# Attention outputs in three fp32r products of halves instead of one fp32 product, in fourteen of sixteen batches

## The reference, cut to what matters

```python
q = softmax_over_the_64_of_a_head(Wq @ layernorm(x)) * SCALE      # 512 x 2048
k = softmax_over_the_2048_columns(Wk @ ctx)                       # 512 x 2048
context = einsum('hdn,hen->hde', k, Wv @ ctx)                     # 64 x 64 per head
out = Wo @ einsum('hde,hdn->hen', context, q) + bo                # 256 x 2048
x = x + out / norm(out, over the 256 rows) * g * sqrt(256)
```

## Time and profile before

| | us |
|---|---|
| median of 3 runs | 2569.74 |
| lowest and highest | 2566.20, 2570.11 |
| profiled execution | 2568.32 |
| its span | 2566.60 |
| mean granted TensorE clock in it | 0.982 of 2.4 GHz |

### The profile page before, as it was taken

How to read it: one execution, slowest core, us unless ns; L and a number is a source line. 1 busy time by engine, 2 the same in 40 slices (tenths; PEclk the granted TensorE clock), 3 DMA queues, 4 the chain that set the end, 5 groups by cost and what they waited for, 6 DMA issues and landing times.

```text
span 2566.6 us, 35379 instructions
## 1 busy us (share of the span) xinstructions
PE 2413.9 (94%) x12004; PEld 1914.3 (75%) x12004; DVE 1726.8 (67%) x4114; ACT 1172.8 (46%) x2464; POOL 1094.4 (43%) x1107
## 2 busy tenths in 40 slices
PE   7999999999999999999999999999999999899774
PEld 6888878887878778787877778777778876777521
DVE  4454567676767557776776567667687756877786
ACT  4454444545354444545444454544445344453333
POOL 1635536172635427262543616245272633623410
PEclk9999999999999999999999999999999999999887
DMA  7112221313122432312213243343302233231376
GB/s 237 50 66 99 74 92 56 108 41 103 63 70 96 128 119 83 113 62 70 95 67 99 80 153 93 120 141 101 123 34 90 92 114 117 76 117 44 88 221 193
DMA packets 200145, 255.72 MB, mean 100 GB/s; under 512 B 43550, under 2 KB 109854, under 8 KB 199966
## 3 DMA queue, kind: packets, MB, share of 16 engines
q1 hardware_dynamic: 199966, 253.47, 31.3%
HBM read 177.53 MB, written 75.89 MB: 99 GB/s over the span
## 4 chain that ended last, share of the span: by engine, by line
PE 57%; DVE 20%; POOL 11%; issue 8%; ACT 3%; SPq 1%; DMA 1%; DVEq 0%; POOLq 0%; ACTq 0%
PE kc_bank L642 15%; PE big L701 7%; PE tb L743 4%; PE tb L757 3%; PE tb L628 3%; PE big L616 3%; PE big L618 3%; PE big L617 3%; POOL x_tr L1535 3%; DVE stats L889 3%; PE big L675 3%; PE big L677 2%; PE big L676 2%; PE tb L686 2%; POOL q_sb L1515 2%
## 5 line engine op out<-in xcount | busy, mean ns | idle before, releaser
L1254 ACT COPY turned<-tb 128x512 f32<-128x512 f32 x512 | 298.7, 587 | 755.3 <-PE tb L686 487.9
L701 PE MATMUL big<-merged,turned 128*128 128x256 f32 x2048 | 495.0, 385 | 36.3 <-ACT turned L1254 24.5
L642 PE MATMUL kc_bank<-ctxt,turned 128*128 128x256 f32 x2048 | 479.5, 380 | 3.0 <-DMA ctxt<-in_ctx_t 3.0
L701 PEld LDWEIGHTS big<-merged,turned 128*128 128x128 f32 x2048 | 385.8, 191 | 110.7 <-ACT turned L1254 19.4
L642 PEld LDWEIGHTS kc_bank<-ctxt,turned 128*128 128x128 f32 x2048 | 374.6, 191 | 54.6 <-issue 8.9
L1490 POOL TENSOR_TENSOR in_l<-x_sb,in_h 128x512 fp32r<-128x512 f32 x128 | 167.8, 1340 | 574.9 <-ACT in_h L1294 574.8
L1515 POOL TENSOR_TENSOR q_sb<-q_sb,qsum 128x1024 f32<-128x1024 f32 x128 | 243.8, 1904 | 274.4 <-DVE qsum L971 274.4
L980 DVE SCALAR_TENSOR_TENSOR on<-big,nrm,g_rows 128x256 f32<-128x256 f32 x256 | 111.9, 479 | 220.7 <-POOL nrm L1528 220.4
L616 PE MATMUL big<-in_h,wk_h 128*128 128x512 f32 x512 | 237.7, 464 | 15.4 <-DVE in_l L821 10.0
L675 PE MATMUL big<-wq_h,in_h 128*128 128x512 f32 x512 | 236.4, 462 | 10.9 <-DVE q_sb L959 10.4
L757 PE MATMUL tb<-mix_ld,mix_w 121*96 121x512 f32 (+2 forms) x324 | 187.9, 677 | 57.7 <-POOL mix_w L1497 28.0
(11 more groups left out here) (149 smaller groups left out, 4308.5 us busy)
## 6 DMA issues: line engine op xcount, KB each, us to landing
mix_ld<-streams SPq DMA_DIRECT2D x157, 240.0 KB
ctxt<-in_ctx_t SPq DMA_DIRECT2D x64, 512.0 KB, 4.0
x_sb<-in_x SPq DMA_DIRECT2D x64, 512.0 KB, 6.1
x_tr<-in_x_t SPq DMA_DIRECT2D x64, 512.0 KB, 6.6
streams<-x_sb SPq DMA_DIRECT2D x64, 512.0 KB, 3.1
stage<-in_ctx SPq DMA_DIRECT2D x60, 512.0 KB, 4.1
out<-mix_out SPq DMA_DIRECT2D x157, 192.0 KB, 2.2
streams<-y_sb SPq DMA_DIRECT2D x32, 256.0 KB, 2.0
```

The source lines that it names most:

```text
L642: t = nc.tensor.matmul(kc_bank[:, 0:C], turned[n % 3][:, j * P:(j + 1) * P], ctxt[:, nt, :], start=nt == 0, stop=nt == NT - 1)
L701: t = nc.tensor.matmul(big[2 + p % 2][:, half], turned[n % 3][:, dt * P:(dt + 1) * P], merged[:, dt, :], start=dt == 0, stop=dt == DT - 1)
L1254: nc.scalar.copy(turned[k % 3][:], tb[n % 2][:]).then_inc(s_tba, 1)
```

## The change

In the first fourteen batches (`SPLIT`) the product of the attention outputs is split. ACT's `turn` writes its copy rounded to fp32r (`turned_h`). DVE's new `query_low` subtracts it from the bank and writes the low half into `q_low`, which lies where `k_exp` lies and of which three quarters are used in turn. `chain_bank` writes a high and a low half of `merged` in three operations instead of one. `attention_out` makes 12 fp32r products of 256 columns instead of 4 in fp32. On DVE `query_low` of tile i−5 stands behind the subtraction of step i; on PE the transposes of tile i−4 now stand ahead of the outputs of tile i−5. A bank with a transposed tile is free once DVE has read it. `key_exp` of the next batch waits for the last outputs, since they read the room of `k_exp`. `pre_t` loses its buffer and uses one of `q_sb`. Batches 14 and 15 go on as before.

```diff
...
+    SPLIT = FIRST[-1]
...
+    LOW_READS = {("fg", b * FG + DT * NQ + i): b * NT + i + 1 for b in range(SPLIT) for i in range(NT)}
...
+        s_low = sem("s_low")
+        s_mrg = sem("s_mrg")
...
-        k_exp = sb("k_exp", [P, N])
-        turned = [sb(f"turned{i}", [P, BANK]) for i in range(3)]
+        with nc.sbuf_tensor("k_exp", [P, N], F32) as k_exp:
+            pass
+        q_low = sb("q_low", [P, 4, BANK], F32R)
+        with nc.sbuf_tensor("turned", [P, 3, BANK], F32) as turned_all:
+            pass
+        turned_h = sb("turned_h", [P, 3, BANK], F32R)
+        turned = [turned_all[:, i, :] for i in range(3)]
...
-        merged = sb("merged", [P, DT, C])
+        with nc.sbuf_tensor("merged", [P, DT, C], F32) as merged:
+            pass
+        merged_h, merged_l = (sb(f"merged_{h}", [P, DT, C], F32R) for h in "hl")
...
-        pre_t = sb("pre_t", [P, COLS])
...
         def f32(ap):
...
+        def low_of(n):
+            return q_low[:, n % 3, :]
+        def pre_t(b):
+            return q_sb[((b + 1) * PAIRS + 2) % QB if b + 1 < NB else QB - 1][:, 0, :]
...
         def wait_read(w, n):
...
-            if name in SCALAR_READS:
+            if name in LOW_READS:
+                w.wait_ge(s_low, LOW_READS[name])
+            elif name in SCALAR_READS:
...
             else:
...
                     else:
...
-                w.wait_ge(s_tba, SCALAR_READS["fg", n])
-                w.wait_ge(s_tbv, VECTOR_READS["chain", b, DT - 1, 2])
-                for dt in range(DT):
-                    t = nc.tensor.matmul(big[2 + p % 2][:, half], turned[n % 3][:, dt * P:(dt + 1) * P], merged[:, dt, :],
-                                         start=dt == 0, stop=dt == DT - 1)
+                bank = big[2 + p % 2][:, half]
+                if b < SPLIT:
+                    w.wait_ge(s_low, LOW_READS["fg", n])
+                    w.wait_ge(s_mrg, 2 * (b + 1) * DT)
+                    for dt in range(DT):
+                        high = turned_h[:, n % 3, dt * P:(dt + 1) * P]
+                        nc.tensor.matmul(bank, high, merged_h[:, dt, :], start=dt == 0, stop=False)
+                        nc.tensor.matmul(bank, high, merged_l[:, dt, :], start=False, stop=False)
+                        t = nc.tensor.matmul(bank, low_of(n)[:, dt * P:(dt + 1) * P], merged_h[:, dt, :], start=False,
+                                             stop=dt == DT - 1)
+                else:
+                    w.wait_ge(s_tba, SCALAR_READS["fg", n])
+                    w.wait_ge(s_tbv, VECTOR_READS["chain", b, DT - 1, 2])
+                    for dt in range(DT):
+                        t = nc.tensor.matmul(bank, turned[n % 3][:, dt * P:(dt + 1) * P], merged[:, dt, :],
+                                             start=dt == 0, stop=dt == DT - 1)
...
             def return_pair(b, p):
...
                         for k in range(KT):
-                            t = nc.tensor.matmul(bank[:], pre_t[:, k * P:(k + 1) * P], wb[:, k, :], start=k == 0,
+                            t = nc.tensor.matmul(bank[:], pre_t(b)[:, k * P:(k + 1) * P], wb[:, k, :], start=k == 0,
...
                     elif task[0] == "mix":
...
                     if i < 2:
...
+                    if 4 <= i < NT + 4 and b < SPLIT:
+                        query_transpose(b, i - 4)
                     if 5 <= i < NT + 5:
...
                     if 10 <= i < NT and i % 2 == 0:
...
-                    if 4 <= i < NT + 4:
+                    if 4 <= i < NT + 4 and b >= SPLIT:
...
                     if b + 1 < NB and i in (17, 19, 21, 23):
...
                 if k == 0:
+                    w.wait_ge(s_mrg, 2 * min(n, SPLIT * DT))
...
                 elif k == 1:
...
                 else:
                     if b:
...
-                    nc.vector.tensor_tensor(merged[:, dt, :], bank[:, 0:C], bo_heads[:], ALU.add).then_inc(s_tbv, 1)
+                    if b < SPLIT:
+                        nc.vector.tensor_tensor(merged_h[:, dt, :], bank[:, 0:C], bo_heads[:], ALU.add).then_inc(s_mrg, 1)
+                        w.wait_ge(s_mrg, 2 * n + 1)
+                        nc.vector.tensor_tensor(chain_t, bank[:, 0:C], f32(merged_h[:, dt, :]), ALU.subtract).then_inc(s_tbv, 1)
+                        w.wait_ge(s_tbv, VECTOR_READS["chain", b, dt, 2])
+                        nc.vector.tensor_tensor(merged_l[:, dt, :], chain_t, bo_heads[:], ALU.add).then_inc(s_mrg, 1)
+                    else:
+                        nc.vector.tensor_tensor(merged[:, dt, :], bank[:, 0:C], bo_heads[:], ALU.add).then_inc(s_tbv, 1)
...
             def key_max(b, dt, i):
...
+            def query_low(b, i):
+                n = b * FG + DT * NQ + i
+                if i == 0:
+                    w.wait_ge(s_tb, TB["fg", n - 1] + 1)
+                w.wait_ge(s_use, n - 2)
+                w.wait_ge(s_tba, SCALAR_READS["fg", n])
+                nc.vector.tensor_tensor(low_of(n), tb[TB["fg", n] % 2][:], f32(turned_h[:, n % 3, :]), ALU.subtract).then_inc(s_low, 1)
             def query_sum(b, p):
...
+                w.wait_ge(s_mrg, 2 * min(b + 1, SPLIT) * DT)
                 if n:
...
                 for j in range(2):
...
                     if i < NT:
...
+                    if b < SPLIT and 5 <= i < NT + 5:
+                        query_low(b, i - 5)
                     if i == 1:
...
                     if i >= 8 and i % 2 == 0 and i < NT + 8:
...
                 if n:
...
+                if b and dt == 0:
+                    w.wait_ge(s_use, b * FG)
...
                 if k >= 3:
...
-                nc.scalar.copy(turned[k % 3][:], tb[n % 2][:]).then_inc(s_tba, 1)
+                if ("fg", k) in LOW_READS:
+                    nc.scalar.copy(turned_h[:, k % 3, :], tb[n % 2][:]).then_inc(s_tba, 1)
+                else:
+                    nc.scalar.copy(turned[k % 3], tb[n % 2][:]).then_inc(s_tba, 1)
...
             def query_exp(b, p):
...
             def pre_out(b, ct):
...
-                nc.scalar.copy(pre_t[:], tb[n % 2][:]).then_inc(s_tba, 1)
+                nc.scalar.copy(pre_t(b), tb[n % 2][:]).then_inc(s_tba, 1)
...
             def y_out(b, ct):
...
```

## The result

| | before | after |
|---|---|---|
| median, us | 2568.18 (4 runs) | 2630.68 (4 runs) |
| lowest and highest | 2566.20, 2570.11 | 2629.41, 2634.49 |
| profiled execution, its span | 2568.32, 2566.6 | 2631.82, 2630.1 |
| mean granted TensorE clock | 0.982 | 0.967 |

The ratio is 1.0246, with a 95% interval of 1.0228 to 1.0264: 62 us more. Forecast was 2597, 29 us more, with 2578 to 2618 as the range of the mechanism that was thought likeliest. The direction holds, and the wait that was named is there; the size is double, because three of its terms were too small.

What follows compares the result with a forecast made beforehand. PE sets the pace with DVE close behind. Twelve batches with Sinkhorn work at 2.7 us late give 32, batches 0 and 1 −3: +29 on 2568.3, so 2597 us; range 2578 to 2618, chance 0.42.

Steps and rivals of the forecast that it cites:

- PE's term: Attention outputs on PE: twelve fp32r matmuls at 0.12 us, 1.44 per tile, saving 0.29 per tile, 65 us if all counts.
- Rival E: The three products on PE are no cheaper; with full weight loads 123 us more than before, 2691; chance 0.04.
- The stage ends 2.7 us late: End of the walk through batch 4's query stage, taken for twelve batches with Sinkhorn work: 12 × 2.7 = 32 us.
- Step 5 … +1.1: Query stage, step 5: operations on merged and the first low half delay the outputs; PE's step ends 1.1 us later.
- I take 7.4: Steps 6 to 9: 7.4 us per pair, between 7.1 and 8.2 with the even stall; PE loses 0.3.
- About +0.3: Steps 10 to 14: DVE 8.45 us per pair against PE's old 8.40; about 0.3 more, late by 1.7.
- Step 15: Step without logits, where PE used to run ahead of DVE and doesn't any more; no cost given.
- low half 14: Steps 16 to 20: it follows second_stats, key_max and a Sinkhorn step on DVE, ends near 720.5; stage 2.7 us late.
- Batches 0 and 1: Query stages where PE stays the bound: 3.2 us saved less 0.4 and 1.3, 1.5 us sooner each, −3 in all.
- B: Rival: VectorE keeps up and the kernel gets faster, 2539, or 2503 with the whole saving; chance 0.32.
- C: Rival: saving and added work cancel, and late outputs 14 are caught up beside the key logits: 2568, within 4; chance 0.12.
- D: Rival: the waits bring TensorE's clock down, 24 to 48 us on top of the forecast, 2621 to 2645; chance 0.10.

Runs made afterwards that it cites:

- e9: Kernel before with only the transposes of tile i-4 put ahead of the outputs of tile i-5, in the first fourteen batches: 2557.7 us.
- e7: Kernel after, but from batch 1 on the low half of merged isn't renewed, one operation per part instead of three: 28 us less.
- e1: Kernel after without the low halves of the queries; the third product reads the high half again: 2568 us.
- e2: Kernel after with low halves made but not read; the outputs wait for ACT alone: 2590 us.
- e10: Kernel before with the outputs of fourteen batches as one fp32r product of high halves, old order, no low halves: gains 50 us.
- e12: Kernel after with unread filler matmuls on PE, sixteen in step 15 and eight in step 19 of batches 2 to 13: 5 us less.
- e14: Kernel after with low half 10 moved to the head of step 15 and low half 14 ahead of second_stats in step 18: 2625 us.

## Why the direction was right and the size wrong

**The accounts of the 62 us.** Order of the transposes −9 (e9), `merged` +28 (e7), DVE's time for the low halves +22, PE's wait for them +41 (e1, e2). What is left to reach e1's +0.5 is 0.5 + 9 − 28 = −18: the cheaper products, where 0.29 × 224 would be 65. This last term is a remainder and takes it that the parts add up. In general they don't: the order alone was worth −9 us on before, nothing in e10 and −70 in after. That PE's time is worth little here has its own evidence in e10's 18% of 280 us and in e12, where 34 us of full-rate time gave 5 to 7.

**PE's term.** The pitch was right. PE in step 8 of batch 4 (start us, us):

```profile
681.63 0.60 PE L709 MATMUL tb<-ident,q_sb 128*128 128x128 f32 x4
683.14 0.38 PE L727 MATMUL big<-merged_h,turned_h 128*128 128x256 f32 x1 [0.91 <-DVE q_low L1015]
683.36 0.28 PE L728 MATMUL big<-merged_l,turned_h 128*128 128x256 f32 x1
...
684.56 0.28 PE L729 MATMUL big<-merged_h,q_low 128*128 128x256 f32 x1
```

Ten matmuls from 683.36 to 684.56 are 0.12 each, the value taken. In batch 0, where nothing holds PE up, a whole step is 3.27 us (from 102.86 to 106.13), against 3.56 before: the 0.29. Rival E falls. The wait of 0.91 ahead of them is three times the 0.29 saved. And there are waits that the list doesn't have, since a matmul's end is modelled: in step 6 the outputs begin 0.58 us behind the transposes (678.12, 678.70), in batch 0 only 0.36, and the low half ends at 678.65.

**DVE's load.** Busy 1879.7 against about 1890, and a low half 0.59 from start to start against 0.57: right.

**The failed step: the walk to "The stage ends 2.7 us late".** It is 5.2 in the mean of batches 2 to 13 and 4.2 in batch 4, whose rows I walked and which is one of the lighter ones. The lateness at the end of a step is how much later than in before PE begins the next step's logits, both counted from the stage's first logits:

```
                  forecast   batch 4   mean 2-13
end of step 5        1.1       2.5       2.4
end of step 9        1.4       4.0       3.4
end of step 13       1.7       4.2       4.6
end of stage         2.7       4.2       5.2
```

The forecast's 1.7 is for the end of step 14, behind which no logits begin. Three terms of the walk were too small: step 5, the pairs of steps 6 to 9, and, in batches other than 4, steps 10 to 14.

First, "Step 5 … +1.1". The outputs of tile 0 begin 3.0 us late, where the walk had 1.7 (663.95 for 662.26), and the step ends 2.5 late. DVE in step 5, after:

```profile
671.77 0.41 DVE L896 TENSOR_TENSOR merged_h<-tb,bo_heads 128x256 fp32r<-128x256 f32 x1
672.22 0.43 DVE L898 TENSOR_TENSOR on<-tb,merged_h 128x256 f32<-128x256 f32 x1
672.68 0.42 DVE L900 TENSOR_TENSOR merged_l<-on,bo_heads 128x256 fp32r<-128x256 f32 x1
```

Two further operations at a pitch of 0.45 are 0.9 per part, and they come twice ahead of the first outputs, for parts 2 and 3. I had counted one of the two in step 5's 1.1 (at 0.75) and put the other at nothing; the walk begins with step 5. But the first transposes of the stage are already 1.1 late: ahead of them PE stands 0.76 us for DVE's copy of a bank of the chain (668.13), which it didn't in before. In e7 the transposes are on time and step 5 ends 0.5 late, so 2.0 of the 2.5 us are these operations, and they stay to the end of the stage (2.2).

Second, "I take 7.4" for the pair of steps, between 7.1 and 8.2. DVE's stalled operation of the odd step in before, then DVE in steps 6 to 8 of after, and POOL beside it:

```profile
668.99 1.72 DVE L1061 TENSOR_TENSOR skw<-skq,ska 128x64 f32<-128x64 f32 x1
```

```profile
676.63 0.69 DVE L993 TENSOR_REDUCE qmax<-big 128x8 f32<-128x512 f32 x1
...
677.97 0.68 DVE L1015 TENSOR_TENSOR q_low<-tb,turned_h 128x512 fp32r<-128x512 f32 x1
678.56 1.24 DVE L1109 TENSOR_TENSOR skw<-skp,skb 128x64 f32<-128x64 f32 x1
...
682.41 0.68 DVE L1015 TENSOR_TENSOR q_low<-tb,turned_h 128x512 fp32r<-128x512 f32 x1
683.00 1.01 DVE L1115 TENSOR_TENSOR skw<-skq,ska 128x64 f32<-128x64 f32 x1
...
684.59 0.69 DVE L993 TENSOR_REDUCE qmax<-big 128x8 f32<-128x512 f32 x1
```

```profile
677.19 1.29 POOL L1568 TENSOR_TENSOR x_pre<-q_sb 128x512 f32<-128x512 f32 x1
678.43 1.28 POOL L1547 TENSOR_TENSOR in_l<-stage,in_h 128x512 fp32r<-128x512 f32 x1
```

From maximum to maximum it is 684.59 − 676.63 = 7.96. Against the 6.53 of the earlier trace rows: two low halves +1.18, the even step's Sinkhorn operation 1.24 instead of 0.21, +1.03, and the odd one 1.01 instead of 1.72, −0.7; other pitches make the last −0.1. The walk also added its 0.3 only once, though steps 6 to 9 are two pairs: by its own numbers it was late by 1.7 there and not by 1.4. The odd half of the reasoning was right: the low half hides in a stall. The even half was the bound that I had named and not taken: a stall of up to 1.1, of which 1.03 came. The low half pushes the Sinkhorn operation from a free moment (666.08 in the earlier trace rows) into an instruction of POOL, and it ends when POOL's does, at 679.7 to 679.8. That could have been seen: in before POOL's halving runs from 666.25 to 667.52, and an operation moved 0.57 later starts at 666.65. The Trainium skill ("SBUF — State Buffer", section "SBUF: two separate sides") calls the shared port a lock for a whole instruction; by that rule a Sinkhorn operation that starts beside such an instruction of POOL is stalled to its end. The trace agrees here.

Third, "About +0.3" for steps 10 to 14. In batch 4 it was about that, in the mean of batches 2 to 13 it was 1.2, and in batches 5, 9 and 13 3 to 4.5. The walk went through one batch only; which wait makes the difference in the others stays open.

**Step 15.** Here I let PE lose its lead over DVE at no price. PE there:

```profile
713.97 0.64 PE L709 MATMUL tb<-ident,q_sb 128*128 128x128 f32 x4
717.78 0.55 PE L727 MATMUL big<-merged_h,turned_h 128*128 128x256 f32 x1 [3.18 <-DVE q_low L1015]
718.13 0.42 PE L728 MATMUL big<-merged_l,turned_h 128*128 128x256 f32 x1
718.35 0.41 PE L729 MATMUL big<-merged_h,q_low 128*128 128x256 f32 x1
```

PE stands for 3.2 us and then runs at a pitch of 0.21 instead of 0.12, with a granted clock of 0.50 (717.7 to 720.4): outputs 10 are 6.7 us late. It is the largest wait to be seen and not the cost: when the last outputs begin 4.7 are left, and with low halves 10 and 14 sooner (e14) or with filler (e12) the kernel gains 5 us each. Of low half 14, to which I had given 1.0 of each batch (from 1.7 to 2.7, which isn't worked out from its rows), the same holds in batches 2 to 13: e14 moves both and the stages end 0.5 sooner. It was no term of its own there.

**Batches 0 and 1:** −0.5 and −0.6, forecast −1.5. Without the operations on `merged` batch 1 stands at −2.6 (e7), so it is the first of the missed terms. The 1.3 that I had given to outputs 14 was right here: with e14 both stages end 1.2 sooner.

**The rivals.** B (VectorE keeps up) would need batches 2 to 13 earlier; they aren't even in e1, without any low half. C (the two cancel) fits e1's time, not after's. D (the clock) has its sign in the profile, 0.96 to 0.98 in the query stages of batches 8 and 4. The measured 2631 lies in D's range, 2621 to 2645, by coincidence: D adds 24 to 48 us to the forecast, and e12 gives back 5 to 7. And not each wait brings the clock down: the one of 1.04 us in the earlier trace rows left it at 1.00 in before, the one of 3.2 in step 15 was followed by 0.50.

**Open.** What makes batches 2 to 13 differ from 3.3 to 7.2. How much of PE's saving the clock takes in e1 and e10. How 22 and 41 us would split if the low halves came at another time. Why the first query stage starts 3.3 us sooner in after's profile (1 to 3 in several other kernels). Whether a low half made by an engine with room would save the 41 us was not tried.

## What to carry to other kernels

When two in-order engines are both nearly full, price a saving on one by a run or window in which it is idle, not by its busy share: here 280 us off PE gave 50, and up to 82 of the rest may have gone to a lower clock. Walk through more than one batch: the one walked here came out at 4.2 us, the mean at 5.2. A new wait of one full queue for another can cost more than the work behind it, here 41 against 22 us, and the largest single wait in the list may be worth next to nothing. When a change bundles edits, look at each alone, and again in the place where it'll stand: the only one here that gains alone is the order of the transposes, 0.56% in all batches; it gives nothing in e10 and 70 us in the kernel after.

## What the runs showed of the hardware

An fp32r matmul of 256 columns takes 0.12 us from start to start at the full clock, 0.21 at 1.2 GHz, and eight fp32 records of the same size took 0.216 each. In batch 4 the clock fell to its lower level (granted 0.50) behind the wait of 3.2 us in step 15 and was back at the next outputs, whose pitch from 721.15 to 722.34 is 0.12 again; over the first 85 us of the stage that was 0.98. A 128x512 operation of DVE with an operand in PSUM runs beside POOL's without being stretched (677.97, 0.68 us, beside 677.19), while one of 64 columns with both in SBUF (678.56, beside 678.43) is stretched from 0.21 to 1.24 us.
